# Two calls instead of one for the second feed-forward product and the experts' last sum, in a fused layer kernel whose engine orders are written out by hand

## The reference

```
h = layernorm(x) * (1 + ca) + sa
h = sqrt(128) * h + pos
4 times:  a = layernorm(h)*s1 + b1;  q, k, v = a@Wq+bq, a@Wk+bk, a@Wv+bv
          h = h + linear_attention(elu(q)+1, elu(k)+1, v) @ Wo + bo          # 16 heads of 8
          h = h + relu((layernorm(h)*s2 + b2) @ W1 + c1) @ W2 + c2           # 512 hidden
x = x + ga * (layernorm(h)*s + b)
g = layernorm(x) * (1 + cb) + sb
x = x + gb * (sum over the top 2 of 8 experts of p_e * (silu(g@G_e) * (g@U_e)) @ D_e  + shared expert)
```

## Time and profile before

| | |
|---|---|
| median of 3 runs | 592.32 us (590.99 to 592.59) |
| the profiled execution | 592.54 us, span from first to last instruction 590.7 us |
| PE busy | 567.1 us (96% of the span), 4578 records |
| DVE, ACT, POOL busy | 432.6 us (73%), 392.6 us (66%), 259.9 us (44%) |
| granted TensorE clock | 1.00 over the whole span |
| one step, from one to the next | 137.8 us |

### The profile page before, as it was taken

The page is one execution under the profiler, slowest core; times in us unless marked ns, Lnnn a source line. Parts: engine busy times, 40 slices in busy tenths (PEclk is TensorE's granted clock), DMA queues, the critical chain, the costliest instruction groups (busy, mean ns, idle before and its releaser), DMA issues.

```text
span 590.7 us, 13153 instructions
## 1 busy us (share of the span) xinstructions
PE 567.1 (96%) x4578; PEld 536.1 (91%) x4578; DVE 432.6 (73%) x1476; ACT 392.6 (66%) x1392; POOL 259.9 (44%) x431
## 2 busy tenths in 40 slices
PE   6999999999999999998999999999999999999997
PEld 4578899998999999998999999998999999999886
DVE  5857667777886776777986777767897666667785
ACT  3777588886666676687594666687675656656651
POOL 4344387554413356553513346745422344435420
PEclk9999999999999999999999999999999999999999
DMA  6800420220000000000000000000000000000000
GB/s 198 235 6 0 159 70 20 102 79 2 19 2 19 2 2 1 2 2 2 2 19 19 1 1 1 2 1 2 2 19 19 1 3 1 1 2 2 1 19 18
DMA packets 11041, 15.58 MB, mean 26 GB/s; under 512 B 968, under 2 KB 8220, under 8 KB 10592
## 3 DMA queue, kind: packets, MB, share of 16 engines
q1 hardware_dynamic: 8896, 12.52, 6.8%
q0 software_dynamic: 448, 1.25, 0.7%
q10 hardware_dynamic: 1632, 0.98, 0.6%
HBM read 12.61 MB, written 2.14 MB: 25 GB/s over the span
## 4 chain that ended last, share of the span: by engine, by line
PE 86%; ACT 4%; POOL 3%; DVE 3%; issue 3%; DMA 1%; SPq 0%; POOLq 0%; DVEq 0%
PE psB L1585 20%; PE psD L1585 20%; PE psC L1585 20%; PE psA L1585 19%; PE psC L1657 1%; PE psA L1657 1%; PE psB L1657 1%; PE psD L1657 1%; DMA wm<-in_wmod 1%; PE psB L1708 1%; PE psC L1708 1%; PE psD L1708 1%; PE psA L1708 1%; ACT kpB L494 0%; ACT xhiC L435 0%
## 5 line engine op out<-in xcount | busy, mean ns | idle before, releaser
L825 POOL TENSOR_TENSOR rstdC<-msC,neghalf 128x2 f32<-128x2 f32 x20 | 14.0, 699 | 89.3 <-ACT eqkC L458 50.3
L825 POOL TENSOR_TENSOR rstdA<-msA,neghalf 128x2 f32<-128x2 f32 x20 | 14.0, 700 | 44.1 <-ACT eqkA L458 40.2
L1585 PE MATMUL psB<-w,H 128*128 128x128 f32 x256 | 31.4, 276 | 0.0
L1585 PE MATMUL psD<-w,H 128*128 128x128 f32 x256 | 31.4, 276 | 0.0
L1585 PE MATMUL psA<-w,H 128*128 128x128 f32 x256 | 31.2, 275 | 0.0
L1585 PE MATMUL psC<-w,H 128*128 128x128 f32 x256 | 31.1, 275 | 0.0
L1585 PEld LDWEIGHTS psC<-w,H 128*128 128x128 f32 x256 | 30.0, 192 | 0.0
L1585 PEld LDWEIGHTS psA<-w,H 128*128 128x128 f32 x256 | 30.0, 192 | 0.0
L1585 PEld LDWEIGHTS psD<-w,H 128*128 128x128 f32 x256 | 29.8, 191 | 0.0
L1585 PEld LDWEIGHTS psB<-w,H 128*128 128x128 f32 x256 | 29.8, 191 | 0.0
L458 ACT ACTIVATE eqkA<-xA 128x129 f32<-128x129 f32 x64 | 19.3, 305 | 15.1 <-DVE xA L1166 7.9
(11 more groups left out here) (576 smaller groups left out, 2366.4 us busy)
## 6 DMA issues: line engine op xcount, KB each, us to landing
M<-modulation_rows SPq DMA_DIRECT2D x2, 1280.0 KB, 7.9
M<-modulation_rows SPq DMA_DIRECT2D x1, 2560.0 KB, 9.2
out<-X SPq DMA_DIRECT2D x16, 128.0 KB, 1.9
M<-in_attn_W SPq DMA_DIRECT2D x3, 256.0 KB, 3.3
X<-in_attn_x_in ACTq DMA_DIRECT2D x2, 256.0 KB, 3.5
M<-in_attn_W ACTq DMA_DIRECT2D x1, 256.0 KB, 3.7
wo<-in_attn_Wo POOLq DMA_DIRECT2D x1, 256.0 KB, 3.7
wm<-in_wmod SPq DMA_DIRECT2D x1, 256.0 KB, 2.8
```

The source lines that it names most:

```text
L825: pool.tensor_tensor(b.rstd[:, :], b.ms[:, :], neghalf[:, :], ALU.pow).then_inc(b.s_rstd.sem, 1)
L1585: return pe.matmul(o, lhsT, rhs, start=start, stop=stop)
```

## The change

`contract(b, i, l)` becomes `contract(b, i, l, k)`, k = 0, 1: chunks 2k and 2k+1, for both token tiles; each call waits for its own `relu` only. `down(b, i)` becomes `down(b, i, part)`: chunks 4, 0, 1 and chunks 2, 3. The sums of both tiles stay open in one bank between the two calls. The number of matmuls, their operands and the semaphore increments are as before. In most places the two calls stand next to each other; other calls stand between those of `contract(A, i, 1)`, `contract(A, i, 2)`, `down(A, i)` and `down(D_, i)`. The lists of calls of ACT, POOL, DVE and PE are ordered anew; each still holds the same calls.

```diff
-            def contract(b, i, l):
-                pe.wait_ge(b.s_h.sem, b.s_h.value(i, (l + 1) * PAIRS))
-                if i == 0:
+            def contract(b, i, l, k):
+
+                pe.wait_ge(b.s_h.sem, b.s_h.value(i, l * PAIRS + k + 1))
+                if i == 0 and k == 0:
                     pe.wait_ge(s_w2, 2 * l + 2)
                 for t in range(TILES):
-                    for c in range(CH):
+                    for c in (2 * k, 2 * k + 1):
                         last = mm(b.ps[:, 0, t * P:(t + 1) * P], b.h[:, c, t * P:(t + 1) * P], w2[:, l, c, :],
-                                  start=c == 0, stop=c == CH - 1)
-                last.then_inc(b.s_w2ps.sem, 1)
+                                  start=c == 0 and t == 0, stop=c == CH - 1 and t == TILES - 1)
+                if k == PAIRS - 1:
+                    last.then_inc(b.s_w2ps.sem, 1)
...
-            def down(b, i):
+            def down(b, i, part):
+                if part == 0:
+                    pe.wait_ge(b.s_units.sem, b.s_units.of(EXPERT_UNITS, "product1", i))
+                else:
+                    pe.wait_ge(b.s_units.sem, b.s_units.of(EXPERT_UNITS, "weighed1", i))
+                for c in ((CH, 0, 1), (2, 3))[part]:
...
```

More of the change, by code:

```diff
@@ L717, in _ @@
                 silu(B, i, 1)
+                if i + 1 < STEPS:
+                    squares(B, i + 1, 1)
                 silu(A, i, 1)
+                tokensT(D_, i)
                 if i + 1 < STEPS:
                     squares(A, i + 1, 1)
-                    squares(B, i + 1, 1)
-                tokensT(D_, i)
                 tokensT(C, i)
@@ L893, in _ @@
-                add_bias(B, i, 3)
                 rstd(A, i, 4)
+                add_bias(A, i, 4)
                 rstd(D_, i, 3)
-                rstd(B, i, 4)
                 add_bias(D_, i, 3)
                 add_bias(C, i, 3)
-                add_bias(A, i, 4)
+                rstd(B, i, 4)
+                if i == 0:
+                    moe_weights()
+                add_bias(B, i, 4)
                 rstd(A, i, 5)
-                add_bias(B, i, 4)
+                add_bias(A, i, 5)
@@ L1330, in _ @@
             masked(B, 0, 0)
-            low(1)
+            scale(D_, 0, 1)
             divided(B, 0, 0)
@@ L1372, in _ @@
                     in_stats(A, i + 1)
+                divided(A, i, 1)
+                positive_keys(B, i, 1)
                 low_part(D_, i, 1)
-                positive_keys(B, i, 1)
-                divided(A, i, 1)
                 move(C, i, 2)
@@ L1380, in _ @@
                     in_stats(B, i + 1)
+                scale(C, i, 3)
                 move(A, i, 3)
@@ L1811, in down @@
                         hid = b.h[:, c, tok] if c < CH else b.hs[:, tok]
-                        last = mm(b.ps[:, 1, tok], hid, wd[:, c, :], start=c == order[0] and t == 0,
-                                  stop=c == order[-1] and t == TILES - 1)
-                last.then_inc(b.s_eps.sem, 1)
+                        last = mm(b.ps[:, 1, tok], hid, wd[:, c, :], start=c == CH and t == 0,
+                                  stop=c == CH - 1 and t == TILES - 1)
+                if part == 1:
+                    last.then_inc(b.s_eps.sem, 1)
             condition()
@@ L1892, in _ @@
                 attend(B, i, 1)
-                contract(D_, i, 0)
+                out_project2(A, i, 1)
+                contract(D_, i, 0, 0)
+                contract(D_, i, 0, 1)
                 out_project(B, i, 1)
@@ L1975, in _ @@
                 attend(A, i, 3)
-                contract(C, i, 2)
-                sums(B, i, 3)
+                transposes(D_, i, 5)
+                contract(C, i, 2, 0)
+                contract(C, i, 2, 1)
                 out_project(A, i, 3)
                 expand(D_, i, 2, 0)
+                sums(B, i, 3)
+                out_project2(A, i, 3)
                 expand(D_, i, 2, 1)
-                out_project2(A, i, 3)
                 attend(B, i, 3)
-                contract(D_, i, 2)
+                contract(D_, i, 2, 0)
+                contract(D_, i, 2, 1)
                 out_project(B, i, 3)
@@ L2004, in _ @@
                 attend(D_, i, 3)
-                contract(B, i, 3)
+                contract(B, i, 3, 0)
+                contract(B, i, 3, 1)
                 out_project(D_, i, 3)
-                logits(A, i)
                 out_project2(D_, i, 3)
                 transposes(C, i, 7)
+                logits(A, i)
                 expand(C, i, 3, 0)
@@ L2026, in _ @@
                 up(B, i, 0)
-                contract(C, i, 3)
+                contract(C, i, 3, 0)
+                contract(C, i, 3, 1)
                 coef_transposes(A, i)
```

377 lines of the change are left out of this document (190 added, 187 removed).

## The result

The changed kernel takes 588.9 us (median of five executions) against 592.32 us: the ratio is 0.9949, 95% interval 0.993 to 0.9967. Four of the five lie at 588.56 to 590.0 us; the fifth took 1125.17 us, is left out of the ratio, and nothing on record explains it. A second series gave 589.39 us, ratio 0.9952 (0.9939 to 0.9966). 588.3 us had been forecast. The profiled execution took 590.0 us, its span is 588.2 us.

What follows compares the result with a forecast made beforehand. PE was taken as the bound: its unchanged records plus about 6 us of pauses per step. 592.54 - 1.4 - 1.5 - 0.45 - 0.7 + 0.05 = 588.54, against the median 588.3 us; range 586.5 to 591.4.

Steps and rivals of the forecast that it cites:

- the split itself: 128 contract and 32 down calls with 80 new waits on PE: taken as 0 cost for each new call.
- experts of A and B, each step: logits2(A) fills the pause before expand(D,0), logits(B) starts 0.30 us earlier: 0.35 us per step, four times.
- experts of C and D begin, each step: Split down(A) lets logits(C) start 0.9 us earlier and the table load move ahead: 0.5 us per step, three times.
- end of C and D, next step's start: transposes(A',1) fills the gap before C's rows; four pairs of transposes end 0.15 us earlier, three times.
- inside the layers, each step: Split and moved calls in the layers: nothing to win and no cost, since PE is the cover.
- last step: Tail, one serial chain: earlier logits(C) removes the pause before logits2(C) and carries what follows, 0.7 us gained.
- step 0, the transfers: GpSimd's moe_weights moved earlier: 0.98 us of pauses gone, a 1.05 us pause new before out_project(D), net cost 0.05.
- step 0, all other moves: Copies of 0.3 to 0.6 us reordered on engines that wait anyway: taken as nothing, 0.5 us to either side.
- GpSimd's root late by 0.3: Experts of A and B: the case behind the term's lower bound, a gain of 0 instead of 0.35 us.
- Rival 3: VectorE's list at the end of C and D late, 1 us in each of 3 steps: 591.3 us; chance 0.07.
- rival 1: Pauses only move to the next serial chain; expert terms shrink from 2.9 to 0.6 us: 591.1 us; chance 0.16.
- a licence for the order: Split of contract in the layers: wins nothing itself, but lets relu(.., 1) come after another copy on ACT.

Runs made afterwards that it cites:

- split_only: The kernel before with contract and down in two calls each and no call moved; 591.7 us, ratio 0.9994 to before.
- low_a_back: The changed kernel with VectorE's low_part(A, 8) put back behind low_part(D, 7) and scale_last(B); 588.35 us, ratio 0.9929 to before.
- trans_back: The changed kernel with transposes(A, 1) behind transposes(C, 0) again at each step's start, on TensorE and ScalarE; 590.5 us, ratio 0.9957 to before.
- experts_new: The kernel before with both splits, and the changed kernel's order only from out_project(D) of layer 3 to the step's end; 589.66 us, ratio 0.9949 to before.
- moe_back: The changed kernel with the seven transfers later on GpSimd, directly ahead of add_bias(D, 4); 593.16 us, ratio 1.0011 to before.
- whole_down: The changed kernel with down as one call again, at the place of its first part; 593.85 us, ratio 1.0027 to before.
- moe_sp: The changed kernel with the seven transfers of the experts' weights issued by SyncE's queue instead of GpSimd; 587.55 us, ratio 0.9917 to before.
- after_again: The changed kernel measured once more, nothing altered; 589.39 us, ratio 0.9952 to before.

## Why the prediction was right, and where not

The mechanism held in the main: the split is free and brings next to nothing by itself, PE's records are the same (the 16 of `contract(C,0)` still take 1.79 us to the next call), and the new order takes pauses out of each step and of the tail. The step is 136.65 us for a forecast 136.8. But one of the terms failed outright, and that the sum still came out is in part luck. Term by term, in us:

| term | predicted | measured | by |
|---|---|---|---|
| the split itself | 0 | 0, or 0.13 each step | split_only, series and trace |
| experts of A and B, each step | 0.35 | 0 | offsets of starts, low_a_back |
| experts of C and D begin, each step | 0.5 | 0.6 to 0.7 | offsets |
| end of C and D, next step's start | 0.15 | 0.3 | offsets, trans_back (0.21) |
| inside the layers, each step | 0 | 0.1 to 0.2 | offsets |
| last step | 0.7 | 0.73 | offsets |
| step 0, the transfers | 0.05 cost | 0 (1.02 lost, 1.05 back) | offsets |
| step 0, all other moves | 0 | 0.4 cost | offset 1.58 at 105 us less 1.22 of the dip |

- **Experts of A and B failed.** "`logits(B)` starts at 275.62" took VectorE's and GpSimd's durations from before and left out that `low_part(A, 8)` had moved ahead of `low_part(D, 7)` and `scale_last(B)`. There it costs twice its time and delays both. `logits(B)` hangs on GpSimd's root for B, which ends at 275.64 us for 274.96 in before: 0.68 us later, of which 0.49 is the kernel's own lateness at this point and 0.19 is new. I had given 0 as a bound, with "GpSimd's root late by 0.3". Putting the call back returned 0.2 us of the 0.35. The rest was in my hops: from the start of guB to `logits(B)` it is 0.66 us in both kernels (275.68 to 276.34, 274.35 to 275.01), for which I had 0.62, and from there to `logits2(B)` 1.55 us, in before 1.49.
- **Experts of C and D were right and a little small.** The table load moved ahead as said and VectorE's own queue became the limit. The exponential starts 1.30 us after the load began, so the 1.28 us of the earlier trace rows held again.
- **The next step's start** showed 0.22 us ahead of `transposes(A',1)` and 0.35 ahead of C's, where 0.4 and 0.1 to 0.2 us were forecast; the swap of A and C was worth 0.21 us a step. Rival 3 (VectorE's list behind `finish(D,0)`) did not occur: no wait stands there. Of rival 1 (the pauses only move) half came true, for the gain of A and B was gone and that of C and D was not.
- **The layers.** That the split is "a licence for the order" was right, and larger than I wrote: without the split of `contract` the new order costs 3.4 us a step more. I had read "none of them waiting in the new lists, the nearest being 0.2 us away" for the split calls; I had not asked what the single call would do, nor expected more than 2 us in all for it.
- **Step 0.** The transfers came out as worked out. The new pause near 78 us is there (at 80.22, with the dip's 1.2 us in it) and the one at 92 us is gone: against before the changed kernel loses 1.02 us at 80 us and gets 1.05 back from 91 to 94. What I costed at nothing, "the other moves of step 0", costs 0.4 us by 50 us: 0.24 of it behind the pause of 0.70 us at 34 us, where `transposes(B,1)` waits for all four first folded matrices, and 0.2 from 46 to 49 us. The 0.5 us that I allowed to either side hold it. The changed kernel's 0.70 us against experts_new are more than that because step 0 of experts_new is itself 0.34 us shorter than that of before.
- **The sum.** Short of it are A and B (1.4 in four steps) and step 0 (0.3); over it are C and D (0.5), the step starts (0.45) and the layers (0.5). These nearly cancel, and that is luck: nothing in the working ties them together. With the dip's 1.22 us taken off, the traces show 3.8 us gained for the 4.0 forecast; the medians without a dip, 592.0 and 588.7 us, show 3.3. The early dip stands in 6 of the changed kernel's 16 executions of both series and in 7 of before's 27 in the second, which moves the medians by some tenths against each other.

## What to carry to other kernels

Price a split product by the order it allows: by itself it may be worth nothing, and the order made for it may be slower than the old one without it. A call moved on an engine with slack still needs a look at what runs beside it (here VectorE beside GpSimd), and at who is queued behind it. A long run of DMA issues on a compute engine is worth moving to a queue that computes nothing (1.0 us here); where it must stay, its place has to be chosen again whenever the list around it changes.

## What the runs showed of the hardware

- A subtraction on VectorE with both inputs in SBUF (128x256) took 806 ns instead of 418 when it began during GpSimd's addition of 128x256, and 411 to 415 ns for the same form of chain C, with no such neighbour. One with an input in PSUM took 0.42 us beside the same addition. A small GpSimd operation (`veB`) that came during the slow one took 0.38 instead of 0.20 us. The Trainium skill (SBUF — State Buffer, SBUF: two separate sides) says that a VectorE operation with two SBUF inputs and a GpSimd operation that reads SBUF hold a common pair of ports in turn, each for its whole duration. The traces agree in which pairs are slowed and, for VectorE's subtraction, roughly in how much: waiting for the addition's end (274.52) and then running for 0.42 us would end at 274.94, the row ends at 274.80. It shows the other way round too: GpSimd's root for A took 0.97 us (294.67 to 295.64) where the same form of subtraction of chain D, which kept its 0.42 us, began at the same time; such a root takes 0.70 us elsewhere.
- In moe_back PE stood idle for 1.30 us, worked for 0.7 us and stood idle for 1.89 us; within the second pause, at 95.7 us, the granted clock fell from 2.4 to 1.2 GHz and stayed there until 102.6 us. The two executions with a mean clock of 0.994 (593.7 and 593.9 us) are 3 us over those of 0.999 and 1.0 (590.8), about as much as the pauses themselves; that their dip is this one and not the early one, no trace shows.
- A dip of the same length (6.8 to 6.9 us) begins at 16 to 17 us in the traces of after, experts_new, moe_back and whole_down, with PE busy throughout from 7 us on, behind a start with a wait of 4.4 us for a transfer. The traces without it (before, moe_sp, trans_back) have the same start and PE as busy up to 17 us; what decides whether it comes, the runs don't show.
- One execution of the changed kernel (after_again) had a mean granted clock of 0.949, evenly over its span, and took 592.74 us, 4.1 over those at full clock; the runs don't show why.
- 80 additional waits on PE whose condition is already met changed the time by a factor of 0.9994 (0.9983 to 1.0005).
